# Attention folds and node scores of a two-layer relational graph network: small products placed as pairs in two column groups of the PE array

## The chip, the cores and the metric

The kernel runs on one NeuronCore of a Trainium2 chip. A core has TensorE (PE in the profile; PEld is its weight load), VectorE (DVE), ScalarE (ACT), GpSimd (POOL), a sync engine that issues transfers (SP) and 16 DMA engines. PE writes to PSUM, eight banks of 128 partitions by 512 f32 words; the other engines copy from there to SBUF. The metric is the device time of one execution in microseconds (us), median of several runs; lower is better.

## The reference

The network has 1250 nodes of 768 features, 20,000 edges with one of three types, and three message-passing layers. Cut to what matters here:

```python
h = relu(layernorm(x));  x = x + gcn(h, W0)               # layer 0
h = relu(layernorm(x))
for each of two attention layers (4 heads, then 1):
    xr = einsum('nd,rdf->rnf', h, W)                      # three relations
    qi = xr[etype, dst] @ q ;  kj = xr[etype, src] @ k    # node scores
    alpha = leaky_relu(qi + kj, 0.2)
    a = softmax of alpha over the edges with the same dst
    h = segment_sum(a * xr[etype, src], dst) + b          # elu after the first
x = x + h
```

The kernel never forms `xr @ q`. It folds the vectors into the weights (`W[r] @ q` and `W[r] @ k`, 768 numbers for each relation and head), and gets the node scores as a product of the node features with the folded vectors. The fold of the first attention layer (four heads) is done on PE; that of the second is done on DVE. In the few words given for the change, the fold is called the second layer's: of the three message-passing layers, the first attention layer is the second.

## The kernel before, in words

Edges are sorted by destination on the chip, in slots of 128, two slots a pair. Nodes are in `NT` = 10 tiles of 128, features in `KT` = 6 blocks of 128. `ps` is all of PSUM as one tile of eight banks. All orders are written out by hand: each engine has its own program, and semaphores link them. Two places matter.

**The fold on PE (lines 1111 to 1136).** Each of three weight matrices (order `FOLDS`) comes in six blocks, in all 18 steps `q`. `turn_block(q)` transposes six 128x128 tiles of a block into PSUM (L1106), ACT copies them to one of two buffers `wt` (L568), and `wq_tile(q)` multiplies (L1135): stationary are 8 columns (query and key vectors, 4 heads each), moving are the 768 columns of `wt` in two halves `h` of 384, one to bank 4 and one to bank 5. PE issues the transposes of `q + 1` ahead of the products of `q`. After six blocks ACT copies both banks' 8 rows to `wqT` (L573), and `fold(r)` transposes that back (L1117). Twelve steps come at the very start, ahead of the first projection; six come in a second stage behind it, just ahead of the first gather loop (L1287).

**The node scores (lines 1239 to 1257).** `by_query(l, g)` takes two tiles of nodes: for each of the six feature blocks it multiplies the 24 folded columns (6 in the second attention layer) with 256 columns of `hT`, and adds up in one bank (L1248). ACT copies the 24x256 result to `qkT` (L637), and `by_node` transposes its two halves (L1257). There are five groups `g` in each attention layer. They stand inside the aggregation loops of the layer before (`to_features`): PE runs the products of node tile `j`, then transposes tile `j - 2`, and at every second tile runs a group of `by_query` first. In the first attention layer `by_node` follows at once, in the second one tile later, save for the last group. The groups 3 and 4 come after the last gather loop.

In these gather loops (L1287 for layer 0, L1353 for the first attention layer) POOL gathers rows to a ring of eight slots, SP relays that they came, DVE writes a one-hot matrix `zw` for a slot (L904, L1083), and PE multiplies it with the row; each step waits for its semaphore.

Every product in float32 with a 128-row contraction shows in the trace as two records of PE and two of PEld: 36 products of L1135 are 72 records, and 60 of L1248 are 120.

Of the kernel before, what the change touches and what calls it, by code (L numbers as in the profile page):

```python
# [15 lines left out]
ACT = mybir.ActivationFunctionType  # L16
# [8 lines left out]
P = 128  # L25
# [3 lines left out]
R = 3  # L29
NT = (N + P - 1) // P  # L30
NP_ = NT * P
KT = D // P
# [5 lines left out]
PAIR = 2 * P  # L38
# [14 lines left out]
QT_BANK, QV_BANK, QV_AT = {1: 4, 2: 6}, {1: 5, 2: 7}, 256  # L53
# [10 lines left out]
HALF = D // 2  # L64
# [18 lines left out]

FOLDS = (2, 1, 0)
NF = 2 * KT


GROUPS_AT = {nt: ((3 * nt,), (3 * nt + 1, 3 * nt + 2)) for nt in range(6)}
# [12 lines left out]
def gnn_kernel(nc, x, src, dst, edge_type, W0, b0, W1, q1, k1, b1, W2, q2, k2, b2, out):  # L101
    HEADS = {1: 4, 2: 1}
# [11 lines left out]
    with ExitStack() as ctx:  # L114
# [6 lines left out]
        ps = ctx.enter_context(nc.psum_tensor("ps", [P, 8, 512], F32))  # L121
# [3 lines left out]
        hT = sb("hT", [P, KT, NP_])  # L125
# [8 lines left out]
        qkT = zw[:, 1, 0, 1:3, :].rearrange("p h c -> p (h c)")  # L134
# [50 lines left out]
        wt = [temp(D) for _ in range(2)]  # L185
        wqT = temp(D, F32, 2 * HEADS[1])
# [15 lines left out]
        wqk = {l: sb(f"wqk{l}", [P, KT, 2, R * HEADS[l]]) for l in (1, 2)}  # L202
        qk1 = sb("qk1", [P, KT, 2, HEADS[1]])
# [55 lines left out]
        wqT_in, wq_folded = sem("wqT_in"), sem("wq_folded")  # L259
# [29 lines left out]
        qt_ready, qt_copied = sem("qt_ready"), sem("qt_copied")  # L289
# [275 lines left out]
        def _(act):  # L565
# [4 lines left out]

            def keep_folded(r):
                act.wait_ge(wt_used, KT * (r + 1))
                nc.scalar.activation(wqT.rearrange("p (a c) -> p a c", a=2), ps[0:2 * HEADS[1], 4:6, 0:HALF], ACT.Copy).then_inc(wqT_in, 1)  # L573

            def keep_transposed(q):
                if q >= 2:
# [41 lines left out]
            for i in range(R):  # L618
                H = HEADS[1]
                c = HALF + i % 2 * KT * 2 * H  # L620
# [13 lines left out]

            def keep_by_query(l, g):
                act.wait_ge(qt_ready, (l - 1) * NT // 2 + g + 1)
                nc.scalar.activation(qkT[0:2 * R * HEADS[l], :], ps[0:2 * R * HEADS[l], QT_BANK[l], 0:PAIR], ACT.Copy).then_inc(qt_copied, 1)  # L637

            for nt in range(NT):
                if nt % 2 == 0 and nt >= 2:  # L640
# [20 lines left out]
            for l in (1, 2):  # L661
# [5 lines left out]
                for r in range(R):  # L667
                    for nt in range(NT):
                        b = nt % 2
# [430 lines left out]
        def _(pe):  # L1100
            mm = nc.tensor.matmul
# [9 lines left out]
            def fold(r):  # L1111

                w = 2 * HEADS[1]
                pe.wait_ge(wqT_in, r + 1)
                for k in range(KT):
                    c = HALF + (r % 2 * KT + k) * w
                    last = nc.tensor.transpose(ps[:, 5 - r // 2, c:c + w], wqT[:, k * P:(k + 1) * P], ident[0:w, 0:w])  # L1117
                last.then_inc(wq_folded, 1)
# [8 lines left out]
            def wq_tile(q):  # L1127
                f = q % KT
                if q == 0:
                    pe.wait_ge(s_qk, 32)  # L1130
                if q == KT:
                    fold(0)
                pe.wait_ge(t_free, (q if q < NF else q + NT) + 1)
                for h in range(2):
                    last = mm(ps[0:2 * HEADS[1], 4 + h, 0:HALF], qk1[:, f, :, :].rearrange("p a h -> p (a h)"), wt[q % 2][:, h * HALF:(h + 1) * HALF], start=(f == 0), stop=(f == KT - 1))  # L1135
                last.then_inc(wt_used, 1)

            def sort_group(g):
# [100 lines left out]
            def by_query(l, g):  # L1239

                if l == 1:
                    pe.wait_ge(wq_copied, R)
                    pe.wait_ge(t_free, NW + NT + 2 * g + 2)
                else:
                    pe.wait_ge(h2_ready, 2 * g + 2)
                w = 2 * R * HEADS[l]
                for k in range(KT):
                    last = mm(ps[0:w, QT_BANK[l], 0:PAIR], wqk[l][:, k, :, :].rearrange("p a q -> p (a q)"), hT[:, k, g * PAIR:(g + 1) * PAIR], start=(k == 0), stop=(k == KT - 1))  # L1248
                last.then_inc(qt_ready, 1)

            def by_node(l, g):
# [42 lines left out]
            for l in (1, 2):  # L1294
# [22 lines left out]
                for r in range(R):  # L1317
# [3 lines left out]
                    for nt in range(NT):  # L1321
                        project(r, nt)
                        for n in MAX_AT.get(r * NT + nt, ()):
                            if n < NT:
# [4 lines left out]
                                for b in range(2):  # L1329
                                    for h in range(H):  # L1330
                                        c = 4 * 512 + (b * H + h) * P
# [53 lines left out]
```

## Time and profile before

| | us |
|---|---|
| median of three runs (1623.75 to 1627.2) | 1625.71 |
| the profiled execution | 1627.17 |
| span in its trace | 1625.4 |
| PE busy | 1477.0 (91%) |
| PE weight loads busy | 879.7 (54%) |
| POOL busy | 998.0 (61%) |
| DVE busy | 901.6 (55%) |
| ACT busy | 271.7 (17%) |

The profile is of one execution. Its busy time of PE counts overlapping records once. A record of a product begins when it starts to stream and ends when its last result is in PSUM, so products that follow each other closely have overlapping records; the step from one to the next is less than the duration of one. Where an instruction waits, its row gives the idle time before it and what ended it.

### The profile page before, as it was taken

The page shows a single profiled execution, that of the slowest core. Times are in us where ns is not written, and L with a number is a line of the kernel's source. Part 1 is how long each engine was busy: PE and PEld are TensorE (multiplying, and loading weights), DVE is VectorE, ACT ScalarE, POOL GpSimd, SP SyncE. Part 2 cuts the span into 40 slices and gives each one's busy share as a digit, 9 for nine tenths or more (in the row PEclk, how much of TensorE's full clock was granted, in tenths as well). Part 3 has the DMA queues.
Part 4 walks back from the last instruction along what each step waited for, and adds up shares of the span by engine and source line. Part 5 has one row for each costly group of instructions (what it writes and reads, how often), then busy time and mean ns, then how long its engine had stood idle before and what let it go on. Part 6 is the DMA issues. An engine that isn't in the chain of part 4 may idle for free.

```text
span 1625.4 us, 24584 instructions
## 1 busy us (share of the span) xinstructions
PE 1477.0 (91%) x6326; PEld 879.7 (54%) x6330; DVE 901.6 (55%) x2002; ACT 271.7 (17%) x696; POOL 998.0 (61%) x1112
## 2 busy tenths in 40 slices
PE   4988999999978999999699999868996999799996
PEld 2554655555556555666455555445553656455553
DVE  8577732334454878888688888505334445223333
ACT  1554310000011333322100123420110001000000
POOL 1489367665527777873277776427656662677673
PEclk9988999999986999899799999968998999899999
DMA  8300399898822122111388888711131111889898
GB/s 305 127 20 21 99 319 306 291 316 294 268 65 66 51 77 82 41 41 41 111 302 288 292 259 258 241 25 31 50 108 31 41 50 50 266 299 306 284 303 265
DMA packets 86810, 271.78 MB, mean 167 GB/s; under 512 B 32156, under 2 KB 32531, under 8 KB 86743
## 3 DMA queue, kind: packets, MB, share of 16 engines
q0 software_dynamic: 51072, 199.44, 39.0%
q1 hardware_dynamic: 34807, 65.62, 11.3%
q10 hardware_dynamic: 864, 5.90, 1.0%
q8 instruction: 34, 0.56, 0.1%
q14 instruction: 33, 0.27, 0.1%
HBM read 239.28 MB, written 31.62 MB: 167 GB/s over the span
## 4 chain that ended last, share of the span: by engine, by line
PE 65%; DMA 11%; POOL 9%; issue 7%; DVE 6%; ACT 1%; DVEq 0%; SPq 0%; POOLq 0%; PEldq 0%; ACTq 0%
PE ps L1353 12%; PE ps L1287 12%; PE ps L1314 12%; DMA ring<-keys,idxr 7%; POOL ring L517 7%; PE ps L1355 6%; PE ps L1356 6%; PE ps L1185 5%; PE ps L1231 3%; DMA ring<-rows,idxr 2%; PE ps L1248 2%; PE ps L1135 2%; PE ps L1106 2%; PE ps L1148 1%; DVE hn L1012 1%
## 5 line engine op out<-in xcount | busy, mean ns | idle before, releaser
L1314 PE MATMUL ps<-wreg,hT 128*128 128x384 f32 x1440 | 484.1, 498 | 7.3 <-PEq L1307 6.6
L517 POOL DMA_INDIRECT ring<-keys,idxr x312 | 323.2, 1036 | 191.4 <-DMA ring<-keys,idxr 72.7
L486 POOL DMA_INDIRECT ring<-rows,idxr x304 | 299.7, 986 | 180.6 <-PEq L1342 66.5
L1314 PEld LDWEIGHTS ps<-wreg,hT 128*128 128x128 f32 x1440 | 279.2, 195 | 200.8 <-issue 21.2
L1353 PE MATMUL ps<-ring,zw 128*128 x664 | 222.2, 493 | 13.0 <-DVE zw L1083 12.6
L1287 PE MATMUL ps<-ring,zw 128*128 x664 | 220.4, 493 | 7.9 <-DVE zw L904 7.9
L486 POOL DMA_INDIRECT ring<-rows,idx x152 | 145.4, 956 | 98.1 <-PE ps L1287 67.3
L1353 PEld LDWEIGHTS ps<-ring,zw 128*128 128x128 f32 x664 | 124.6, 191 | 104.9 <-issue 29.8
L1081 DVE TENSOR_TENSOR ring<-ring,al x166 | 159.0, 958 | 36.4 <-SPq L404 24.7
L1287 PEld LDWEIGHTS ps<-ring,zw 128*128 128x128 f32 x664 | 126.6, 192 | 96.3 <-issue 13.9
L1086 DVE TENSOR_SCALAR zw<-iota_f,tl,al 128x128 f32<-128x128 f32 x166 | 61.5, 372 | 155.8 <-PE ps L1356 133.3
L1355 PE MATMUL ps<-ring,zw 128*128 x332 | 137.3, 496 | 10.1 <-DVE zw L1086 10.1
L904 DVE TENSOR_SCALAR zw<-iota_f,tl,ring 128x128 f32<-128x128 f32 x166 | 58.5, 358 | 158.5 <-PE ps L1287 135.4
L471 POOL TENSOR_SCALAR stT<-iota_h,stT 125x128 f16<-125x128 f16 x160 | 106.6, 685 | 56.2 <-PE ps L1150 28.2
L1356 PE MATMUL ps<-ring,zw 128*128 x332 | 135.9, 491 | 0.0
L1012 DVE TENSOR_TENSOR hn<-al,hn 128x1024 f32 x83 | 101.7, 1225 | 38.1 <-POOL al L535 14.5
L1018 DVE TENSOR_TENSOR hn<-hn,al 128x256 f32 x83 | 35.6, 429 | 142.2 <-POOL al L535 126.2
L1015 DVE TENSOR_TENSOR zw<-zw,hn 128x1024 f32<-128x1024 f32 x83 | 101.7, 1226 | 2.9
L1355 PEld LDWEIGHTS ps<-ring,zw 128*128 128x128 f32 x332 | 62.6, 192 | 54.6 <-issue 16.1
L1356 PEld LDWEIGHTS ps<-ring,zw 128*128 128x128 f32 x332 | 63.7, 192 | 44.8 <-issue 1.5
L1185 PE MATMUL ps<-ring,hT 128*128 128x384 f32 x240 | 87.8, 522 | 0.0
L684 ACT ACTIVATE stage<-ps 128x384 f32<-128x384 f32 x60 | 29.5, 491 | 276.8 <-PE ps L1314 276.8
(189 smaller groups left out, 1363.4 us busy)
## 6 DMA issues: line engine op xcount, KB each, us to landing
wreg<-in_L_gnn_W SPq DMA_DIRECT2D x11, 2304.0 KB, 9.7
rows<-stage SPq DMA_DIRECT2D x30, 386.0 KB
rows<-stage SPq DMA_DIRECT2D x30, 384.5 KB, 2.8
stT<-targets_row ACTq DMA_DIRECT2D x6, 960.0 KB
ring<-keys,idxr POOLq DMA_INDIRECT x312, 2.4
ring<-rows,idxr POOLq DMA_INDIRECT x304, 4.6
rows<-stT SPq DMA_DIRECT2D x10, 384.0 KB, 2.8
xs<-in_x SPq DMA_DIRECT2D x3, 1152.0 KB, 13.1
```

The lines of the kernel that those rows point to most:

```text
L471: nc.gpsimd.tensor_scalar(oh_tg[:, c % PB, :], iota_h[0:EP, 0:P], dloc[:, c:c + 1], None, ALU.is_equal).then_inc(tg_in, 1)
L486: nc.gpsimd.indirect_dma_start(ring[:, t % (2 * RING), 0:WIDTH[l]], None, rows[l], bass.IndirectOffsetOnAxis(idx[:, t:t + 1], 0)).then_inc ...
L517: nc.gpsimd.indirect_dma_start(kb[:, n % KSEMS, t % KB, 0:4], None, keys[l], bass.IndirectOffsetOnAxis(idxr[:, t:t + 1], 0)).then_inc(k_in ...
L1012: V.tensor_tensor(scored[:, :, 0:H, :], scores_at(i, 0, H, 2).rearrange("p (b h) -> p b h", b=2).unsqueeze(3).to_broadcast([P, 2, H, P]), ...
L1015: V.tensor_tensor(run, run, scored[:, :, 0:H, :], ALU.max).then_inc(m_chain[l], 1)
L1081: V.tensor_tensor(row, row, scores_at(i, b, H).unsqueeze(2).to_broadcast([P, H, ROW // H]), ALU.mult).then_inc(rows_scaled, 1)
L1185: last = mm(ps[:, 4 - 2 * (nt % 2) + h, 0:HALF], hT[:, k, nt * P:(nt + 1) * P], w0s[:, k, h * HALF:(h + 1) * HALF], start=(k == 0), stop=( ...
L1287: last = mm(ps[:, 2 * (j % 2) + a, 0:HALF], zw[:, 0, b, 0, :], row_at(i, b, a * HALF, (a + 1) * HALF), start=False, stop=False, skip_group ...
L1314: last = mm(ps[:, 2 * (nt % 2) + h, 0:HALF], hT[:, k, nt * P:(nt + 1) * P], wreg[:, r % 2, k, h * HALF:(h + 1) * HALF], start=(k == 0), st ...
L1353: last = mm(ps[:, 2 * (j % 2) + a, 0:2 * W], zw[:, 0, b, 0, :], row_at(i, b, a * 2 * W, (a + 1) * 2 * W), start=False, stop=False, skip_gr ...
L1355: mm(ps[:, 2 * (j % 2), 0:HALF], zw[:, 0, b, 0, :], row_at(i, b, 0, HALF), start=False, stop=False, skip_group_check=True)
L1356: last = mm(ps[:, 2 * (j % 2) + 1, 0:HALF + 1], zw[:, 0, b, 0, :], row_at(i, b, HALF, D + 1), start=False, stop=False, skip_group_check=True)
```

## The change

The two products of each pair now write different partitions of PSUM, and so lie in different groups of columns of the PE array: the first at partition 0, the second at 64. In the fold these are the two halves of 384 columns, which exist already. In the node scores the one product of 256 columns becomes two of 128, one for each node tile. All other products keep their place. As a consequence the two ACT copies can't take both results in one instruction: L573 and L637 each become two of half the width. The copy of the folds now signals after each half, and `fold` waits for both; the copy of the scores signals once, after its second half. The built program showed a 32-column tile of the array for these products before too, at position 0; now half of them are at column 64.

```diff
+QK_AT = (0, 64)
+WQ_AT = (0, 64)
...
             def keep_folded(r):
                 act.wait_ge(wt_used, KT * (r + 1))
-                nc.scalar.activation(wqT.rearrange("p (a c) -> p a c", a=2), ps[0:2 * HEADS[1], 4:6, 0:HALF], ACT.Copy).then_inc(wqT_in, 1)
+                for h in range(2):
+                    nc.scalar.activation(wqT[:, h * HALF:(h + 1) * HALF], ps[WQ_AT[h]:WQ_AT[h] + 2 * HEADS[1], 4 + h, 0:HALF], ACT.Copy).then_inc(wqT_in, 1)
...
             def keep_by_query(l, g):
-                nc.scalar.activation(qkT[0:2 * R * HEADS[l], :], ps[0:2 * R * HEADS[l], QT_BANK[l], 0:PAIR], ACT.Copy).then_inc(qt_copied, 1)
+                for b, c in enumerate(QK_AT):
+                    last = nc.scalar.activation(qkT[0:2 * R * HEADS[l], b * P:(b + 1) * P], ps[c:c + 2 * R * HEADS[l], QT_BANK[l], 0:P], ACT.Copy)
+                last.then_inc(qt_copied, 1)
...
             def fold(r):
-                pe.wait_ge(wqT_in, r + 1)
+                pe.wait_ge(wqT_in, 2 * (r + 1))
...
                 for h in range(2):
-                    last = mm(ps[0:2 * HEADS[1], 4 + h, 0:HALF], ...
+                    last = mm(ps[WQ_AT[h]:WQ_AT[h] + 2 * HEADS[1], 4 + h, 0:HALF], ...
...
                 for k in range(KT):
-                    last = mm(ps[0:w, QT_BANK[l], 0:PAIR], wqk[l][:, k, :, :].rearrange("p a q -> p (a q)"), hT[:, k, g * PAIR:(g + 1) * PAIR], start=(k == 0), stop=(k == KT - 1))
+                    for b, c in enumerate(QK_AT):
+                        last = mm(ps[c:c + w, QT_BANK[l], 0:P], wqk[l][:, k, :, :].rearrange("p a q -> p (a q)"), hT[:, k, (2 * g + b) * P:(2 * g + b + 1) * P], start=(k == 0), stop=(k == KT - 1))
```

On PE, the first group of node scores of the first attention layer, between two gather loops (`hT` holds node features, `wqk` folded vectors, `hn` normalised nodes), before:

```order
L1248 MATMUL ps<-hT,wqk 24x256 x6
L1257 MATMUL ps<-ident,zw 128x24 x2
L1277 MATMUL ps<-ident,hn 128x128 x6
L1211 MATMUL ps<-zero 128x8 x2
L1283 UNCONDITIONAL_BRANCH
```

and now:

```order
L1254 MATMUL ps<-hT,wqk 24x128 x12
L1263 MATMUL ps<-ident,zw 128x24 x2
L1283 MATMUL ps<-ident,hn 128x128 x6
L1216 MATMUL ps<-zero 128x8 x2
L1289 UNCONDITIONAL_BRANCH
```

Six products have become twelve of half the width; nothing else has moved on PE. The fold's products keep their count and shape there.

On ACT, the first stage of the folds (`stT` holds `wt` and `wqT`), before:

```order
L568 ACTIVATE stT<-ps 128x768 x7
L573 ACTIVATE stT<-ps 8x768
L568 ACTIVATE stT<-ps 128x768 x5
L573 ACTIVATE stT<-ps 8x768
L568 ACTIVATE hT<-ps 128x6x128 x2
```

and now:

```order
L570 ACTIVATE stT<-ps 128x768 x7
L576 ACTIVATE stT<-ps 8x384 x2
L570 ACTIVATE stT<-ps 128x768 x5
L576 ACTIVATE stT<-ps 8x384 x2
L570 ACTIVATE hT<-ps 128x6x128 x2
```

Each copy of a folded result is two instructions; all others stand where they stood.

## Rows read from the trace of the kernel before

**Rows 1.** The page: span, and the lines of the chain that ended last.

```profile
span 1625.4 us, 24584 instructions
...
PE ps L1353 12%; PE ps L1287 12%; PE ps L1314 12%; DMA ring<-keys,idxr 7%; POOL ring L517 7%; PE ps L1355 6%; PE ps L1356 6%; PE ps L1185 5%; PE ps L1231 3%; DMA ring<-rows,idxr 2%; PE ps L1248 2%; PE ps L1135 2%; PE ps L1106 2%; PE ps L1148 1%; DVE hn L1012 1%
```

**Rows 2.** Line 1135: records, ns minimum/median/maximum, first and last start, forms.

```profile
L1135 PEld LDWEIGHTS ps<-stT,qk x72: 85/90/138, 20.8 to 214.2; 128*8 128x8 f32 x72
L1135 PE MATMUL ps<-stT,qk x72: 486/486/847, 20.8 to 214.5; 128*8 128x384 f32 x72
```

**Rows 3.** Timeline of a fold step: start us, us, engine, line, operation, [idle before].

```profile
24.40 1.46 PE L1135 MATMUL ps<-stT,qk 128*8 128x384 f32 x4
24.73 0.09 PEld L1135 LDWEIGHTS ps<-stT,qk 128*8 128x8 f32 x1 [0.23 <-issue]
25.79 0.87 PE L1106 MATMUL ps<-ident,wreg 128*128 128x128 f32 x6
```

**Rows 4.** Windows: stretch, length, busy PE, PEld, DVE, ACT, POOL, granted clock, DMA.

```profile
37.00:41.00 4.00, 4.00 (x14) 1.55 (x13) 3.79 (x11) 1.61 (x2) 0.00 (x0) 0.57 0.02 6
```

**Rows 5.** Timeline at the end of the first fold stage.

```profile
46.21 1.26 DVE L827 TENSOR_SCALAR hn<-xs,mv,rstd 128x768 f32<-128x768 f32 x2
...
53.22 0.80 ACT L573 ACTIVATE stT<-ps 8x768 f32<-8x768 f32 x1 [1.80 <-PE ps L1135]
54.08 0.54 PE L1117 MATMUL ps<-ident,stT 8*128 8x8 f32 x6 [0.89 <-ACT stT L573]
54.54 0.88 PE L1106 MATMUL ps<-ident,hn 128*128 128x128 f32 x6
```

**Rows 6.** Timeline at the end of the second fold stage.

```profile
202.05 0.27 ACT L613 ACTIVATE tlT<-ps 128x128 bf16<-128x128 f32 x1
202.21 0.26 ACT L614 ACTIVATE tlT<-ps 52x128 bf16<-52x128 f32 x1
...
214.73 0.60 DVE L904 TENSOR_SCALAR zw<-iota_f,tl,ring 128x128 f32<-128x128 f32 x2 [4.46 <-SPq L404]
...
216.40 6.05 PE L1287 MATMUL ps<-ring,zw 128*128 x18
```

**Rows 7.** Line 1248 between 366 and 560 us: records as in Rows 2.

```profile
L1248 PEld LDWEIGHTS ps<-hT,wqk x60: 98/103/103, 371.8 to 471.0; 128*24 128x24 f32 x60
L1248 PE MATMUL ps<-hT,wqk x60: 376/379/397, 371.8 to 471.2; 128*24 128x256 f32 x60
```

**Rows 8.** Timeline around group 1 of the first attention layer's scores.

```profile
409.31 2.77 PE L1248 MATMUL ps<-hT,wqk 128*24 128x256 f32 x12
...
411.62 0.59 DVE L904 TENSOR_SCALAR zw<-iota_f,tl,ring 128x128 f32<-128x128 f32 x2
...
413.54 1.86 PE L1287 MATMUL ps<-ring,zw 128*128 x5
```

**Rows 9.** Timeline around group 2.

```profile
441.94 0.60 DVE L904 TENSOR_SCALAR zw<-iota_f,tl,ring 128x128 f32<-128x128 f32 x2 [2.32 <-SPq L404]
442.45 2.84 PE L1287 MATMUL ps<-ring,zw 128*128 x8 [0.74 <-DVE zw L904]
...
449.45 3.79 PE L1287 MATMUL ps<-ring,zw 128*128 x11
...
451.27 0.35 DVE L904 TENSOR_SCALAR zw<-iota_f,tl,ring 128x128 f32<-128x128 f32 x1 [3.71 <-SPq L404]
```

**Rows 10.** Timeline behind group 0 of the second attention layer, and of groups 3 and 4.

```profile
968.14 1.66 ACT L708 ACTIVATE etmp<-ps,b1c 128x128 f32<-128x128 f32 x6 [0.43 <-PE ps L1277]
...
1051.35 4.32 PE L1248 MATMUL ps<-hT,wqk 128*6 128x256 f32 x12 [5.03 <-DVE hT L1062]
...
1053.02 0.14 PEld L1248 LDWEIGHTS ps<-hT,wqk 128*6 128x6 f32 x1 [0.29 <-issue]
1053.45 0.14 PEld L1248 LDWEIGHTS ps<-hT,wqk 128*6 128x6 f32 x1 [0.29 <-issue]
...
1066.54 5.25 PE L1248 MATMUL ps<-hT,wqk 128*6 128x256 f32 x12 [9.03 <-DVE hT L1062]
```

More of the change, by code:

```diff
@@ L1134, in wq_tile @@
                 for h in range(2):
-                    last = mm(ps[0:2 * HEADS[1], 4 + h, 0:HALF], qk1[:, f, :, :].rearrange("p a h -> p (a h)"), wt[q % 2][:, h * HALF:(h + 1) * HALF], start=(f == 0), stop=(f == KT - 1))
+                    last = mm(ps[WQ_AT[h]:WQ_AT[h] + 2 * HEADS[1], 4 + h, 0:HALF], qk1[:, f, :, :].rearrange("p a h -> p (a h)"), wt[q % 2][:, h * HALF:(h + 1) * HALF], start=(f == 0), stop=(f == KT - 1))
                 last.then_inc(wt_used, 1)
```

## The prediction

> **What bounds the kernel now.** I read the chain that ended last first. Its lines give L1248 and L1135, the two lines that the change touches, 2% of the span each [rows 1]. That is some 32 us each of 1625.4 with the rounding (1.5 to 2.5% would be 24 to 40), and about all the time these lines stream, so nearly every changed product stands on the path. Then the records of each line [rows 2, 7], for the step from one product to the next, and the timeline at both ends of each stage, for what is late once PE comes sooner. In the fold a step of q takes 24.40 to 25.79 for four records and then the transposes [rows 3]: PE waits for nothing but its own order there, and ACT's copy lies beside it.
>
> **The unit.** A fold record takes 486 ns [rows 2] but the next begins 0.33 us behind it (24.40 to 24.73, the load that goes with it [rows 3]); the rest is the fill of the array and lies under its follower. So the four records of a step of q are 4 x 0.325 = 1.30 us. In the node scores twelve records take 2.77 us with one of them 379 ns [rows 7, 8]: (2.77 - 0.38) / 11 = 0.217 us a step.
>
> **What two column groups can save.** The trace of before shows no product at column 64, so this is bounded from both sides. One end: nothing overlaps, saving 0. Other end: each pair takes the time of one product, saving half of all streaming. I take a value between, from how a float32 product is made up: two records, on the same column group. I assume that products start in the order in which they are issued and that two on one column group can't stream together. With A and B the two groups, the order is A1 A2 B1 B2. A2 waits for A1, B1 starts with A2, B2 waits for B1. A lone pair then takes three units in place of four; a row of pairs takes two units a pair, plus one at its end, since the next A1 goes beside B2. No row here shows it; it is nearer to the full end for the scores than for the folds.
>
> The Trainium skill, "TensorE: Matmul & The Clock Gate", section "Part 3: Packing small matmuls", says that products in different column groups run together, that they start and end in program order, and that a packed set takes one product's duration and some 4 ns for each further tile. Taken for whole float32 products it gives the full end, which is a rival below; its statement on order is what I assume, and no run here has shown either yet.
>
> **First fold stage, 12 steps.** Eight lone steps at full clock save one unit: 8 x 0.325 = 2.6. The first step and the one after PE's pause at 36 us run at about half clock (0.57 granted in that window [rows 4], the longest record 847 ns [rows 2]), with a unit of twice 0.325, so 0.65; but if the clock rises at the same moment as now, the transposes behind it get the slow time instead, which leaves 0.33. I take 0.45 each, 0.9. The last two steps stand together with a short wait for ACT in between: 0.6. Together 4.1. The two folded copies become two each: 8x768 took 0.80 us [rows 5]. Two back-to-back ACT copies of 128 columns start 0.16 us apart and last 0.27 [rows 6], so a split costs about 0.05 (bounds: 0 by overlap, 0.26 by the longest spacing in the trace for such a width, 1.66 us for six [rows 10]). 4.1 - 0.1 = 4.0. What is late next: the transposes of `hn` at 54.54, whose input DVE began at 46.21 and had at 47.5 [rows 5]. So a shift of up to 7 us passes on. Behind it the sort and the first projection are linked to PE through semaphores on each column, so all of it moves by the same 4.0.
>
> **Second fold stage, 6 steps.** They would save 4 x 0.325 + 0.6 - 0.05 = 1.85. But the gather loop waits for DVE's one-hot: that began at 214.73 [rows 6], and PE's first use of such a one came 0.51 us after its start at 441.94 [rows 9]. So PE can't start before 215.24, and now does at 216.40 [rows 6]: 1.15 counts.
>
> **Node scores of the first attention layer, 5 groups.** Before 12 x 0.217 = 2.60. Now 24 records of half the unit: 13 x 0.108 = 1.41, saving 1.19. A floor of issue stands against this: six tiny products at L1117, each with a load, take 0.54 us, less 0.2 for the last one's fill (my estimate), so 0.066 each [rows 5]; 24 x 0.066 = 1.6, saving 1.0. I take 1.1. Cover ahead: at group 1 DVE's one-hot started at 411.62 and is usable at 412.13, PE starts at 413.54 [rows 8]: room for 1.4. Group 0 stands alike. At group 2 the third slot's one-hot starts only at 451.27, held by the gather, so it is usable at 451.78; PE gets to it at 449.45 + 8 x 0.325 = 452.05 [rows 9]: only 0.3 counts. Groups 3 and 4 have no loop behind them. 4 x 1.1 + 0.3 = 4.7, less five split copies of 0.06: 4.4.
>
> **Node scores of the second attention layer.** Groups 0 to 2 lie in the loop at full clock, and their copies are read one tile later, so are free: 3.3. Group 3 takes 4.32 and group 4 5.25 us, as PE had idled (5.03 and 9.03 us) and its step is 0.43 us, 1053.02 to 1053.45, the lower of its two clock levels [rows 10]. Now 13 x 0.214 + 0.17 = 2.95 each. Group 3 saves 1.4 less 0.3 for transposes behind it that come before the clock rises: 1.1. Group 4 saves 2.3, less 0.06: 2.2. Sum 6.6.
>
> **Sum.** 4.0 + 1.15 + 4.4 + 6.6 = 16.2 us off the profiled execution's 1627.17 (span 1625.4 and 1.8 around it), so 1611.0. That execution stands 1.5 above the median of the runs; the same saving from 1625.71 gives 1609.6, the forecast. Its own range is 1602 to 1616.
>
> The Trainium skill, "TensorEngine Tiling (Array Packing)", section "Key Properties", has a change of tiling mode drain the array. The 0.17 us of idle that PE's loads show between transposes and fold products would be such a change and stays, since the mode was the same before; so the sum is the same by it.
>
> **Rivals.**
> (a) Every product's two records overlap with the other product's, the full end. Folds then save two units a step (about 8.2 in the first stage, still 1.15 in the second by its cap), scores 0.1 more a group: about 21.5 saved, 1604. For it: nothing in the trace says that a second record must wait. Against it: same-group records step at 0.33 now. 0.07.
> (b) The overlap works, but the gather loops give the time back, PE meeting rows that haven't come. For it: group 2's slack of 0.3, one-hots held by SP's relay [rows 9]. Against it: 1.4 of room at group 1 [rows 8]. Then the five groups inside the loops give nothing (3.3 and 2.5 lost): 10.4 saved, 1615. 0.11.
> (c) Nothing overlaps: two products that both read all 128 rows stream one after the other. The change then doesn't do what it is said to do; 24 half steps take what 12 did. Left are the split copies, 3 x 0.05 and 6 x 0.06 = 0.5, at most nine of 0.26 = 2.3: 1626.2 to 1628. For it: no row shows an overlap. 0.17.
> (d) Slower: weight loads of one column group can't run under products of the other. Now each load of 103 ns [rows 7] hides under a product on its own group; if it stood free, a group of scores would take 24 x (0.108 + 0.103) = 5.1 in place of 2.6, +2.5 in eight groups, and +3.4 in the two at the low clock (24 x (0.214 + 0.14) = 8.5 against 5.1); a fold step +4 x 0.09 = 0.36 [rows 2], 18 times. 20 + 6.8 + 6.5 + 0.5 = 34 slower, 1659. It decides from 0.05 us of exposed load on each record of the scores, where 24 of them eat the 1.19 saved. For it: the loads double in number while the streams halve. Against it: 103 ns would still fit under a stream of 108. 0.15.
> The same page's section "Part 3: Packing small matmuls" has loads overlap with products in flight only where the row group differs, and here both groups use all rows: that is this rival. For a single column group the trace disagrees, as loads start under running products at 24.73 [rows 3].
>
> **Chances.** Forecast 0.50, (a) 0.07, (b) 0.11, (c) 0.17, (d) 0.15. I call faster or slower what differs by over 0.2% (3.3 us), about what a measurement of this kernel can tell from no change: faster 0.68 (the forecast, (a) and (b)), same 0.17, slower 0.15. The range is 1602 to 1628: it takes in (b) and (c) and leaves out (d) and the far end of (a).
>
> **What would show it.** In the profile after, the four records of a lone fold step lie within about 1.14 us from first start to last end in place of 1.46, and the second and third start together; a score group is about 1.6 to 1.75 long in place of 2.77 with 24 records of some 270 ns; the first gather loop starts some 5 us sooner; PE's busy time falls by more than 15 us. Score groups over 2.7 us long would make the prediction wrong by (c), loads with idle time between them and products by (d). If the groups are short but the aggregation loops longer by as much, it is (b).

## The result, and the profile after

The changed kernel took 1606.98 us in the median of four runs (1604.7 to 1619.93), beside 1626.45 for the kernel before (four runs): ratio 0.9891, 95% interval 0.9861 to 0.9921. Run again later beside 11 runs of the kernel before it came to 1608.81 (six runs, 1602.91 to 1613.88) against 1622.92: 0.9913, 0.9886 to 0.994. So it is faster, by 19.5 us the first time and 14.1 the second, by the medians; the forecast was 1609.6. Executions of one program here spread over 10 us and more (29 runs of the kernel before: 1620.12 to 1634.32), so a trace and a median can differ by several us.

The page of the changed kernel, to compare with [rows 1]:

```profile
span 1605.3 us, 24837 instructions
...
PE 1453.7 (91%) x6446; PEld 878.0 (55%) x6450; DVE 901.0 (56%) x2002; ACT 274.0 (17%) x709; POOL 1000.9 (62%) x1112
...
PE ps L1293 12%; PE ps L1320 12%; PE ps L1359 12%; DMA ring<-keys,idxr 8%; POOL ring L519 8%; PE ps L1361 6%; PE ps L1362 6%; PE ps L1190 5%; DMA ring<-rows,idxr 3%; PE ps L1111 1%; PE ps L1236 1%; PE ps L1153 1%; PE ps L1254 1%; DVE zw L1020 1%; DVE hn L1017 1%
```

PE is busy 23.3 us less. The fold line (L1140 now) has left the list of the chain and the score line (L1254 now) has gone from 2% to 1%. The records of both lines, against [rows 2] and [rows 7] (the first two of the fold, the next two of the scores between 350 and 480 us; ns minimum/median/maximum):

```profile
L1140 PEld LDWEIGHTS ps<-stT,qk x72: 85/88/95, 20.8 to 204.0; 128*8 128x8 f32 x72
L1140 PE MATMUL ps<-stT,qk x72: 486/489/847, 20.8 to 204.3; 128*8 128x384 f32 x72
```

```profile
L1254 PEld LDWEIGHTS ps<-hT,wqk x120: 98/103/103, 367.3 to 458.3; 128*24 128x24 f32 x120
L1254 PE MATMUL ps<-hT,wqk x120: 269/273/290, 367.3 to 458.4; 128*24 128x128 f32 x120
```

A fold record is as long as it was; loads are too. What changed is when they start. The timeline of a fold step, against [rows 3], and under it the same step asked for up to 25.0 us only:

```profile
24.95 0.10 PEld L1140 LDWEIGHTS ps<-stT,qk 128*8 128x8 f32 x4 [0.17 <-issue]
24.95 0.82 PE L1140 MATMUL ps<-stT,qk 128*8 128x384 f32 x4
...
25.70 0.87 PE L1111 MATMUL ps<-ident,wreg 128*128 128x128 f32 x6
```

```profile
24.95 0.49 PE L1140 MATMUL ps<-stT,qk 128*8 128x384 f32 x2
```

All four loads lie in the first 0.10 us, two records have started by 25.0 (at 24.951 and 24.957) and the other two follow a unit of 0.325 later (25.276 and 25.283): 2 x 0.325 + 0.17 = 0.82, in place of 1.46. The overlap is full. It is not that the second product waits for the first to reach its second record, as I had assumed: it starts ahead of it.

Scores, group 1 of the first attention layer, against [rows 8]:

```profile
401.96 1.50 PE L1254 MATMUL ps<-hT,wqk 128*24 128x128 f32 x24
...
403.51 0.55 ACT L641 ACTIVATE zw<-ps 24x128 f32<-24x128 f32 x2 [15.88 <-PE ps L1254]
404.11 0.30 PE L1263 MATMUL ps<-ident,zw 24*128 24x24 f32 x2 [0.65 <-ACT zw L641]
...
404.27 0.59 DVE L909 TENSOR_SCALAR zw<-iota_f,tl,ring 128x128 f32<-128x128 f32 x2
...
405.10 1.21 PE L1293 MATMUL ps<-ring,zw 128*128 x3
```

24 records take 1.50 us, twelve units of 0.11 and the fill. The gather loop's products begin 3.14 us behind the group's start, before 4.23 [rows 8]: 1.1 us saved. PE waits for the copy 0.65 us, 0.2 more than before (0.46).

What the trace shows of the stages, as PE reaches them (before / after, us): transposes of `hn` 54.54 / 50.93; end of the sort and projection (the two transposes ahead of the second fold stage) 201.46 / 194.71; first gather loop 216.40 / 208.51; score group 0 371.82 / 367.26; score group 1 409.31 / 401.96; last group 468.81 / 457.19; group 3 of the second attention layer 1051.35 / 1034.81; end 1625.4 / 1605.3. PE gains 3.6, then 3.1 more in the sort, 1.1 in the second fold stage; then it loses 3.3 in the first gather loop. Group 0 of the scores is reached 4.6 us sooner, and 15.5 are gained behind it. Not all of that is the change's: from group 0 to group 1 PE gains 2.8 us, of which group 0 itself gives 1.1. The same interval before, now, and in the kernel with column groups in the scores alone (below):

```profile
371.82:409.31 37.49, 34.96 (x120) 20.24 (x119) 15.69 (x37) 2.00 (x3) 21.95 (x23) 0.95 0.88 293
```

```profile
367.26:401.96 34.70, 32.00 (x131) 19.59 (x130) 15.09 (x35) 2.16 (x4) 21.39 (x23) 1.00 0.91 312
```

```profile
368.69:405.07 36.38, 33.67 (x131) 20.33 (x130) 15.72 (x37) 2.16 (x4) 21.44 (x23) 0.95 0.89 299
```

At the same granted clock of 0.95 the interval is 1.11 us shorter, as the group's saving has it; the other 1.7 us go with a clock of 1.00, and what set it in that execution is open.

The loss of 3.3 us has a cause in the rows. Windows (columns as in [rows 4]) of the first 10 us of the first gather loop, before and after:

```profile
216.40:226.40 10.00, 10.00 (x33) 5.97 (x34) 2.53 (x7) 0.42 (x3) 7.10 (x9) 1.00 0.90 301
```

```profile
208.50:218.50 10.00, 9.99 (x23) 5.67 (x23) 1.74 (x6) 0.00 (x0) 5.81 (x7) 0.72 0.82 255
```

Before, PE came from the folds straight into the loop, at full clock. Now it comes early, waits 1.99 us for the first one-hot, and starts at the lower of its two levels: 23 records in place of 33. All traces of this study agree: the three kernels with the folds as before have 33 or 34 records and a granted clock of 1.00 in these 10 us, and the seven executions with column groups in the folds and nothing put into the wait have 22 to 27 records and 0.69 to 0.85.

The first fold stage shows the same twice over. PE's rows around its pause, before and after:

```profile
30.97 1.46 PE L1135 MATMUL ps<-stT,qk 128*8 128x384 f32 x4
36.62 0.87 PE L1106 MATMUL ps<-ident,wreg 128*128 128x128 f32 x6 [4.18 <-issue]
37.41 2.73 PE L1135 MATMUL ps<-stT,qk 128*8 128x384 f32 x4
40.08 1.21 PE L1106 MATMUL ps<-ident,wreg 128*128 128x128 f32 x6
```

```profile
28.06 0.82 PE L1140 MATMUL ps<-stT,qk 128*8 128x384 f32 x4
34.34 1.54 PE L1111 MATMUL ps<-ident,wreg 128*128 128x128 f32 x6 [5.47 <-issue]
...
42.27 1.42 PE L1140 MATMUL ps<-stT,qk 128*8 128x384 f32 x4
43.61 0.88 PE L1111 MATMUL ps<-ident,wreg 128*128 128x128 f32 x6
```

The pause has grown from 4.18 to 5.47 us. Before, the first six transposes behind it were still fast (0.87 us), and the low clock lay between 37.4 and about 41 us. Now it begins with the transposes at 34.34 (1.54 us) and lasts to about 43. The line of the register loads says what the pause is (PE's sequencer, ns as above), before and after:

```profile
L344 PEldq TENSOR_LOAD <-bounds x10: 294/304/482, 29.9 to 36.0; - x10
```

```profile
L346 PEldq TENSOR_LOAD <-bounds x10: 294/302/494, 27.7 to 33.7; - x10
L346 PEldq FUSED_REGOPS  x10: 146/146/165, 28.2 to 34.1; - x10
```

Ten loads of the tile bounds, each with what goes with it, take 6.6 us of sequencer time (27.7 to 34.3 now, 29.9 to 36.5 before), some 0.66 us each. They begin while the array still has work queued: 2.5 us ahead of the end of its products before (32.43), 1.2 us now (28.88). So shorter products hide less of them: 2.3 us of the 3.5 that the five steps ahead of the pause had won pass on.

### The profile page after: what moved, and what is told of

It is laid out like the page before. It is cut to its first block, busy times and chain, and to the rows that moved or that the text cites. A ratio compares the mean times of both kernels' runs of the same rounds, so it can differ in the third digit from the quotient of the medians.

```text
span 1605.3 us, 24837 instructions
## 1 busy us (share of the span) xinstructions
PE 1453.7 (91%) x6446; PEld 878.0 (55%) x6450; DVE 901.0 (56%) x2002; ACT 274.0 (17%) x709; POOL 1000.9 (62%) x1112
## 4 chain that ended last, share of the span: by engine, by line
PE 61%; DMA 14%; POOL 10%; issue 7%; DVE 5%; ACT 1%; DVEq 1%; SPq 0%; POOLq 0%; ACTq 0%; PEldq 0%
PE ps L1293 12%; PE ps L1320 12%; PE ps L1359 12%; DMA ring<-keys,idxr 8%; POOL ring L519 8%; PE ps L1361 6%; PE ps L1362 6%; PE ps L1190 5%; DMA ring<-rows,idxr 3%; PE ps L1111 1%; PE ps L1236 1%; PE ps L1153 1%; PE ps L1254 1%; DVE zw L1020 1%; DVE hn L1017 1%
## 5 line engine op out<-in xcount | busy, mean ns | idle before, releaser
L519 POOL DMA_INDIRECT ring<-keys,idxr x312 | 319.2, 1023 | 189.1 <-DMA ring<-keys,idxr 73.6
L488 POOL DMA_INDIRECT ring<-rows,idxr x304 | 303.7, 999 | 168.8 <-PEq L1348 60.9
L1017 DVE TENSOR_TENSOR hn<-al,hn 128x1024 f32 x83 | 101.7, 1225 | 35.4 <-POOL al L537 15.5
L1023 DVE TENSOR_TENSOR hn<-hn,al 128x256 f32 x83 | 35.6, 429 | 143.8 <-POOL al L537 127.8
L659 ACT ACTIVATE hn<-iota_f,tlb 128x128 f32<-128x128 f32 (+1 forms) x166 | 56.8, 393 | 119.2 <-DVE hn L1017 105.7
```

The costliest lines, as they stand in the source:

```text
L488: nc.gpsimd.indirect_dma_start(ring[:, t % (2 * RING), 0:WIDTH[l]], None, rows[l], bass.IndirectOffsetOnAxis(idx[:, t:t + 1], 0)).then_inc ...
L519: nc.gpsimd.indirect_dma_start(kb[:, n % KSEMS, t % KB, 0:4], None, keys[l], bass.IndirectOffsetOnAxis(idxr[:, t:t + 1], 0)).then_inc(k_in ...
L1017: V.tensor_tensor(scored[:, :, 0:H, :], scores_at(i, 0, H, 2).rearrange("p (b h) -> p b h", b=2).unsqueeze(3).to_broadcast([P, 2, H, P]), ...
```

## The experiments

### Each half of the change alone

`e1_folds` has the column groups in the folds alone, `e2_scores` in the scores alone. `e2_scores` has the fold lines of the kernel before; the edit of `e1_folds` against the changed kernel is:

```diff
-                for b, c in enumerate(QK_AT):
-                    last = nc.scalar.activation(qkT[0:2 * R * HEADS[l], b * P:(b + 1) * P], ...)
-                last.then_inc(qt_copied, 1)
+                nc.scalar.activation(qkT[0:2 * R * HEADS[l], :], ps[0:2 * R * HEADS[l], QT_BANK[l], 0:PAIR], ACT.Copy).then_inc(qt_copied, 1)
...
-                    for b, c in enumerate(QK_AT):
-                        last = mm(ps[c:c + w, QT_BANK[l], 0:P], ...)
+                    last = mm(ps[0:w, QT_BANK[l], 0:PAIR], ...)
```

> Column groups in the folds alone; node scores as before. Theory (the overlap is full, two records of A with two of B, and what it saves passes on): a fold step stays 0.82 us of PE, the score groups are back at 2.77. The first stage gives 3.6 us earlier transposes of hn, the second is cut by the wait for the first one-hot and by the low clock behind that wait, so 4 to 9 us faster than before in all (the 20 us of the whole change less 11 to 13 for the scores). Rival (the folds' saving is lost in the sort, and the scores make up the gain): within 2 us of before.

> Column groups in the node scores alone; folds as before. Theory: each group 1.50 us in place of 2.77, about 1.05 saved net of the longer wait for ACT in the five of the first attention layer, 1.27 in three of the second, 1.6 and 2.3 in the last two: 5.3 + 3.8 + 3.9 = 13 us faster at most, 10 to 13. Rival (gather loops give back what is saved inside them): 6 to 8 us.

Measured: folds alone 1623.32 us (12 runs) against 1625.63 of the kernel before (29 runs), ratio 0.9991 (0.9975 to 1.0008): 2.3 us by the medians, at most 4.1 by the interval, and not told from nothing. Scores alone 1612.89 (6 runs): 0.9927 (0.9906 to 0.9948), 12.7 us. Together 15, which agrees with the 14.1 of the second measurement of the whole. So the scores carry nearly all of the gain. My range of 4 to 9 us for the folds was too high but for its lowest end; the rival's size, within 2 us or so, fits. Its reason, that the sort eats the saving, does not (see the pause below).

The same loss at the start of the gather loop is seen here: `hn` is transposed 5.1 us sooner than before in the profiled execution (49.45 us), and the loop's first 10 us have a low clock (26 records in place of 33):

```profile
209.80:219.80 10.00, 9.99 (x26) 5.84 (x27) 2.19 (x7) 0.00 (x0) 6.83 (x9) 0.84 0.89 300
```

Single traces do not place the rest of what is missing. Over the five executions with two column groups in the folds, the pause in place and nothing put into the waits, group 0 of the scores starts at 368.2 us in the mean (366.6 to 370.9), over the three with the folds as before at 371.6 (368.7 to 374.2): 3.4 us sooner, with a spread as large. So part of the folds' saving seems to be left there, and 2.3 us and 3.4 us can't be told apart.

### Is it the overlap, or the shorter product?

```diff
                 for k in range(KT):
-                    last = mm(ps[0:w, QT_BANK[l], 0:PAIR], wqk..., hT[:, k, g * PAIR:(g + 1) * PAIR], ...)
+                    for b in range(2):
+                        last = mm(ps[0:w, QT_BANK[l], b * P:(b + 1) * P], wqk..., hT[:, k, (2 * g + b) * P:(2 * g + b + 1) * P], ...)
```

> The kernel before with the node scores split into twelve products of 128 columns, all in the one column group at partition 0, side by side in the bank, with one ACT copy. Theory (the gain is the overlap of two column groups): no gain, a group takes 24 x 0.108 + 0.17 = 2.77 us, as with twelve records of 0.217, total within 2 us of before. Rival (the shorter products are the gain, since fill and loads hide better): groups clearly under 2.77 us. Rival (a short product exposes its load): groups of 24 x 0.2 = 5 us, 20 us slower.

This kernel leaves out part of the score sums (the sums of both halves lie in one bank at the same partitions); instructions and shapes are those intended. It took 1628.26 us (10 runs), ratio 1.0008 (0.9987 to 1.0029). A group:

```profile
374.17 2.80 PE L1249 MATMUL ps<-hT,wqk 128*24 128x128 f32 x24
```

2.80 us for the same 24 records that take 1.50 in two column groups. Halving the product costs nothing and gains nothing; the column group is what gains. It also prices rival (c): had nothing overlapped, the time would have stayed.

### Does the order of issue matter?

```diff
-                for k in range(KT):
-                    for b, c in enumerate(QK_AT):
+                for b, c in enumerate(QK_AT):
+                    for k in range(KT):
```

> The whole change, but each score group issues its six products of column group 0 first, then the six of column group 64, in place of taking turns. Theory (products start in the order of issue, and two overlap only where neighbours in that order lie in different groups): only the one pair at the seam overlaps, a group takes 11 product times, 22 x 0.108 + 0.17 = 2.55 us or more, and total is about 11 us slower than the changed kernel. Rival (PE picks products of a free column group out of its queue): groups stay at 1.50 us and the total is that of the changed kernel, 1607.

1623.61 us (10 runs), ratio 0.9978 (0.996 to 0.9997): 2.0 us under the kernel before that was measured beside it, where the changed kernel was 14.1 under its own. So some 12 us are lost, nearly all of the scores' gain. A group:

```profile
370.93 2.39 PE L1254 MATMUL ps<-hT,wqk 128*24 128x128 f32 x24
```

The loads between 371.815 and 371.83 alone; two begin there within 2 ns (371.818 and 371.820):

```profile
371.82 0.10 PEld L1254 LDWEIGHTS ps<-hT,wqk 128*24 128x24 f32 x2
```

2.39 us. Against 2.80 without overlap that is 0.41, or four records of 0.109 that overlap at the seam. I had expected two. The starts show how: eight records stand alone, 0.11 us apart; the first of the second set starts at 371.822, 6 ns behind the ninth of the first set (371.816), and the last three of the first set only follow at 371.925, 372.035 and 372.144. So PE took products of the free column group ahead of some that had to wait, but only over a few records: products that are to overlap have to stand next to each other. The Trainium skill, "TensorE: Matmul & The Clock Gate", section "Part 3: Packing small matmuls", has products start strictly in program order; this trace does not agree, by those three records. Nor does the lone fold step, where the second product starts 0.32 us ahead of the first one's second record.

### Four column groups in the folds

```diff
-WQ_AT = (0, 64)
+WQ_AT = (0, 32, 64, 96)
+QUART = D // 4
...
-                for h in range(2):
-                    last = mm(ps[WQ_AT[h]:WQ_AT[h] + 2 * HEADS[1], 4 + h, 0:HALF], ...)
+                for h in range(4):
+                    last = mm(ps[WQ_AT[h]:WQ_AT[h] + 2 * HEADS[1], 4 + h // 2, h % 2 * QUART:(h % 2 + 1) * QUART], ...)
```

> The changed kernel once more, beside the next three on one chip, since its first result had four runs only. Theory of additive parts: folds alone gave about 2 us and scores alone about 12.5, so this gives 14 to 16 us less than before, 1610 to 1612. Rival (the parts help each other, as the first four runs had it): 19 less, 1607.

> The changed kernel with the folds' 768 columns in four quarters of 192, at columns 0, 32, 64 and 96, and four ACT copies. Theory (groups overlap freely up to four, but what PE saves in the folds now meets waits: ten register loads in the first stage, the first one-hot and a low clock in the second): a fold step takes 0.50 us in place of 0.82, and the total stays within 2 us of the changed kernel. Rival (a third and fourth group don't overlap, moving data being the limit): the step stays 0.82. Rival (what folds save counts): 4 us or more faster than the changed kernel.

The changed kernel came to 1608.81, as the additive theory had it. Four groups in the folds came to 1604.3 (6 runs), ratio 0.9878 (0.9853 to 0.9902), against 0.9913 (0.9886 to 0.994) of the changed kernel. The intervals overlap, so 4.5 us is the best guess and not shown; neither the theory (within 2 us) nor the rival (4 us or more) is decided. The step is 0.51 us as expected, and the wait for the first one-hot grows:

```profile
207.05 0.51 PE L1141 MATMUL ps<-stT,qk 128*8 128x192 f32 x8 [0.52 <-ACT stT L571]
209.04 0.80 PE L1123 MATMUL ps<-ident,stT 8*128 8x8 f32 x6 [1.48 <-ACT stT L577]
...
213.12 1.64 PE L1294 MATMUL ps<-ring,zw 128*128 x2 [3.12 <-DVE zw L910]
```

3.12 us of wait in place of 1.99, and 1.48 for the four copies in place of 1.09.

### The pause in the first fold stage

```diff
-                if q == KT:
-                    bnd = load_bounds(pe)
...
                     last.then_inc(p_ready, 1)
+                    if h == 0:
+                        j = nt + 1
+                        pe.wait_ge(bounds_ready, 1)
+                        bnd.append(pe.value_load(bounds[0:1, j:j + 1], ...))
```

> The changed kernel with PE's ten register loads of the tile bounds moved from the middle of the first fold stage to behind the products of each of the ten node tiles' first half in the projection, where PE's sequencer runs ahead of the array. Theory (the pause of 5.5 us, 28.9 to 34.3, is the sequencer's ten loads of 0.64 us, and the low clock until 43.6 follows from it): no pause, transposes of hn start when DVE's hn is there, at 47.5 to 48, in place of 50.9, so 3 us faster in total at most. Rival (the pause is the wait for the second weight matrix): it stays. Rival (the sort takes up the difference): total as the changed kernel.

The pause is gone, so it was the loads. But the total is 1610.43 (6 runs), ratio 0.9923 (0.9898 to 0.9947): no gain over the changed kernel is seen, though the intervals would hide one of 3 us. PE:

```profile
41.99 0.54 PE L1122 MATMUL ps<-ident,stT 8*128 8x8 f32 x6 [1.09 <-ACT stT L576]
46.91 1.54 PE L1111 MATMUL ps<-ident,hn 128*128 128x128 f32 x6 [4.38 <-DVE hn L832]
```

The folds are done 8.5 us sooner, then PE waits 4.38 us for `hn` and enters the sort at the low clock, 1.54 us for six transposes in place of 0.88. `hn` at 46.91 is 4.0 us sooner than at 50.93, and the end of the sort is at 195.94, 1.2 later. The sort stage in four traces, by windows from the transposes of `hn` to its end:

```profile
54.54:201.46 146.92, 133.08 (x624) 78.70 (x623) 100.48 (x371) 70.67 (x189) 103.89 (x153) 0.91 0.16 57
```

```profile
50.93:194.71 143.78, 130.32 (x625) 76.54 (x624) 100.48 (x371) 70.66 (x189) 103.75 (x153) 0.93 0.16 58
```

```profile
46.91:195.94 149.03, 135.18 (x622) 80.35 (x623) 104.16 (x388) 70.72 (x189) 103.73 (x153) 0.89 0.13 46
```

```profile
54.36:198.04 143.68, 130.25 (x625) 76.50 (x624) 100.48 (x371) 70.63 (x189) 103.74 (x153) 0.93 0.17 58
```

These are the kernel before, the changed one, this one (where some of DVE's earlier work falls into the stage, 388 instructions in place of 371), and scores alone, whose sort and folds are those of the kernel before. Length goes with the granted clock: 0.93, 0.91, 0.89. The last row shows that the 3.1 us which the changed kernel's trace gained in the sort is not the change's: a kernel without column groups in its folds had them too.

The other traces say more. With the folds as before the stage took 143.7, 146.9 and 149.4 us in three kernels; with two column groups in them, and the pause in place, 143.7 to 143.8 (four executions), 146.6 to 146.7 (three) and 149.5 (one). The same three lengths come in both, so the sort does not take up what the folds save. Over these eight executions `hn` is transposed at 50.30 us in the mean (48.95 to 51.26), over the three with the folds as before at 54.34 (54.12 to 54.54): 4.0 us sooner. What sets the clock of an execution in the sort I did not test; it stays open.

### Keeping PE busy in its waits

```diff
             wq_tile(NW - 1)
+            def fill(n):
+                for _ in range(n):
+                    mm(ps[:, 6, :], zero16[:, 0:P], zero16[:, 0:512], start=True, stop=True)
+            fill(4)
             fold(R - 1)
+            fill(8)
```

> The changed kernel with products of zeros in PE's two waits ahead of the first gather loop: 4 of 512 columns while ACT copies the fold, 8 more while the first one-hot is awaited (0.215 us each at full clock, to a bank nobody reads). Theory (the low clock behind that wait, granted 0.72 in the first 10 us, cost 2.7 us of the folds' saving): granted clock near 1.00 there, 2 to 2.7 us faster in total. Rival (the gather is the limit at the loop's start): clock up, total the same.

> The filler kernel once more, since it came out 8 us under the changed kernel of the same call where its trace accounts for 2.6 (in the first 10 us of the gather loop 31 records in place of 23). Theory (the rest was chance between executions): 1605 to 1607 here. Rival (it was real): 1600 to 1601.

The first 10 us of the gather loop now:

```profile
208.00:218.00 10.00, 9.92 (x31) 5.96 (x32) 2.95 (x8) 0.00 (x0) 7.57 (x8) 1.00 0.94 327
```

Full clock, and 31 records in place of 23: 8 x 0.325 = 2.6 us, the expected size. From its first product to score group 0 the loop takes 155.7 us here and 155.8 in the repeat, 158.75 in the changed kernel and 155.42 in the kernel before: the loss of 3.3 us is undone but for 0.3. So the low clock was its cause, and the waits were what it followed. In total 1600.43 (5 runs), ratio 0.9867 (0.984 to 0.9893), and again 1602.29 (6 runs), 0.9876 (0.9846 to 0.9906), measured at another time. That is 6.5 to 8.4 us under the changed kernel's 1608.81, of which the trace accounts for 2.6 to 3.0. The repeat fell between my two expectations. The ratios' intervals reach the changed kernel's, so what the rows show stands and the rest does not.

The second set of fillers stands in the waits ahead of the last two score groups:

```diff
+                if l == 2 and g >= 3:
+                    pe.wait_ge(divided, 9)
+                    fill_tail({3: 32, 4: 64}[g])
...
+                if l == 2:
+                    fill_tail(12)
                 pe.wait_ge(q16_ready, l)
```

> The filler kernel with more products of zeros (256 columns, to a bank nobody reads) in PE's long waits ahead of groups 3 and 4 of the second attention layer's scores (32 and 64) and behind the last (12). Theory (these groups take 2.73 us in place of 1.50 only for the low clock, and transposes and the next products of zeros after them are slow too): groups 1.50 us each, 1.2 + 1.2 us, 1.2 to 2 for what stands behind them: 3 to 4 us faster than the filler kernel. Rival (the fillers delay ACT or PE by as much): no gain.

In the changed kernel, and then in this one (in both, the first row is group 3):

```profile
1034.81 2.73 PE L1254 MATMUL ps<-hT,wqk 128*6 128x128 f32 x24 [5.01 <-DVE hT L1067]
1037.47 1.54 PE L1283 MATMUL ps<-ident,hn 128*128 128x128 f32 x6
```

```profile
1030.13 1.48 PE L1268 MATMUL ps<-hT,wqk 128*6 128x128 f32 x24 [1.52 <-DVE hT L1067]
1031.54 0.88 PE L1297 MATMUL ps<-ident,hn 128*128 128x128 f32 x6
...
1033.27 7.15 PE L1253 MATMUL ps<-zero 128*128 128x256 bf16 x64
1042.45 1.82 PE L1268 MATMUL ps<-hT,wqk 128*6 128x128 f32 x24 [2.03 <-DVE hT L1067]
...
1048.18 2.28 PE L1228 MATMUL ps<-zero 128*128 128x512 bf16 x5 [0.22 <-issue]
```

Group 3 and its transposes are fast. Group 4 gets 1.82 us; a wait of 2.03 was left ahead of it. The 12 fillers behind it ran at the low clock (2.74 us, where 32 had taken 3.66), and what follows starts 5.73 us behind the group's start, 5.72 in the changed kernel: what the group saved is lost there. In total 1600.75 (6 runs), ratio 0.9862 (0.9833 to 0.9891), 1.5 us under the filler kernel measured beside it: half of what I expected, and within the spread.

### Four column groups in the scores, and all together

```diff
-QK_AT = (0, 64)
+QK_AT = (0, 32, 64, 96)
...
                     for b, c in enumerate(QK_AT):
-                        last = mm(ps[c:c + w, QT_BANK[l], 0:P], ...)
+                        last = mm(ps[c:c + w, QT_BANK[l], 0:P // 2], wqk..., hT[:, k, (4 * g + b) * P // 2:(4 * g + b + 1) * P // 2], ...)
```

> The changed kernel with the score groups in four products of 64 columns at columns 0, 32, 64 and 96, and four ACT copies of 64 columns. Theory (up to four groups overlap, and 96 records with their loads can still be issued at under 10 ns each): a group takes 12 x 0.055 + 0.17 = 0.83 us in place of 1.50, less 0.2 us of longer copies where PE waits for them: 4 to 6 us faster than the changed kernel's 1608.8. Rival (loads bind: with 24 columns each and four at once they can't hide under 54 ns of stream): group stays near or above 1.5 us, no gain or slower.

> All of it together: four column groups in folds and scores, and both sets of fillers. Theory (each saves what its trace shows, and the fills keep the clock up): 1593 to 1598. Rival (four groups give nothing more, as their savings turn into waits): the same as with fillers alone and two groups.

Four groups in the scores: 1598.12 us (6 runs), ratio 0.9841 (0.9811 to 0.9871), 10.7 under the changed kernel's 1608.81 of another time, where I expected 4 to 6. A group (six feature blocks of four products, so 48 records and not the 96 that I wrote):

```profile
368.92 0.87 PE L1254 MATMUL ps<-hT,wqk 128*24 128x64 f32 x48
369.96 0.90 ACT L641 ACTIVATE zw<-ps 24x64 f32<-24x64 f32 x4 [16.68 <-PE ps L1254]
370.91 0.30 PE L1263 MATMUL ps<-ident,zw 24*128 24x24 f32 x2 [1.12 <-ACT zw L641]
```

0.87 us in place of 1.50, and loads of 24 columns still hide. PE waits 1.12 us for the copies in this group and 1.01 or 1.02 in later ones, in place of 0.65. So where the transposes follow at once a group gains 0.16 to 0.26 net, and 0.63 in three others; the two slow groups of the second attention layer (1.47 us each in place of 2.73) gain 1.3 and 0.9. By these rows all groups give some 5 us, so part of the 10.7 is spread again. That this kernel is faster than the changed one is shown, as the intervals of the ratios lie apart (0.9871 and 0.9886), though measured at two times.

All together came to 1595.31 us (6 runs, 1592.22 to 1603.39), ratio 0.9843 (0.9811 to 0.9875): the lowest median of this study, 28.7 us under the kernel before measured beside it (25.5 by the ratio), and faster than both kernels of the document. Over four groups in the scores alone it isn't proved (the ratios are the same). In the trace of all together PE still waits 1.69 us for the first one-hot behind the fillers, and the next 10 us have a granted clock of 1.00 and 31 records.

## Why the prediction was right

**Time and side.** 1609.6 forecast, 1606.98 and 1608.81 measured; own range 1602 to 1616. The forecast's case came true: groups overlap, and the time falls. That the sum came within 3 us is partly luck, as its parts were off in both directions: folds 5.15 forecast and 2.3 measured alone, scores 11.0 and 12.7, and the overlap itself was fuller than assumed.

**Where the changed lines stand.** Reading the two lines' shares of the chain as "nearly all of it on the path" was right for the scores (12.7 us passed on of the 13 that their rows gave at most). For the folds it was right of their time, but waits and a low clock took part of its place.

**The unit.** Wrong: the step "A2 waits for A1, B1 starts with A2", and the premise under it, that products start in the order of issue. The two products start 0.01 us apart and their second records follow together, so a lone pair takes two units, not three. That is the full end, rival (a), to which I gave 0.07. A fold step saved 0.64 us, twice the 0.325 of the sum.

**First fold stage, 4.0.** The trace has 3.6, and eight executions 4.0 in the mean, but as two errors that cancel. Full overlap would have given about 8; the pause took 1.3 (4.18 to 5.47 us), the low clock from 34 to 43 us most of the rest. I had counted the pause as fixed in length, where the loads in it are: what was queued ahead of them hid 2.5 us and now hides 1.2. The split of the folded copy cost 0.2 us (a wait of 1.08 or 1.09 in place of 0.89), not 0.05.

**The sort moves with it.** Single traces can't show it, as the stage differs by up to 6 us with the granted clock (0.90 to 0.93), more than the shift itself. But it took the same three lengths with either kind of folds, so nothing speaks against it.

**Second fold stage, 1.15.** 14.94 us before and 13.80 now from end of sort to first gather product: 1.14. The cap by DVE's one-hot was right. What I did not see is the price behind it, a wait of 1.99 us that put PE to its lower clock and cost 2.6 to 3.0 us, as the filler kernel shows. With it the second stage loses. So the folds' 5.2 us were mis-sized, 2.3 measured (0.9991, interval 0.9975 to 1.0008).

**Scores of the first attention layer, 4.4.** Up to the gather loop's next product group 1 saves 1.09, with 1.27 on PE and 0.2 of longer wait for ACT (I had 1.1 and 0.06). The floor of issue of 0.066 us a record did not hold: 24 records in two groups start some 0.053 us apart (1.50 us less the 0.27 of the last one, over 23), and 48 in four groups 0.014 (0.87 less 0.2, over 47). The cap of 0.3 at group 2 did not show either: from it to group 3 took 16.45 us before and 15.35 now (445.22 to 461.67, 435.77 to 451.12), and the third slot's one-hot, which the gather held to 451.27, now starts at 440.73 behind a wait for PE alone. The trace's 7.1 us between group 0 and the last are more than these groups' own 4.4, 1.7 of it by the clock of one interval as said above.

**Scores of the second attention layer, 6.6.** Group 3 saves 1.6 and group 4 2.5 (4.32 and 5.25 us in [rows 10], 2.73 each now) against 1.4 and 2.3; the transposes behind group 3 cost 0.66 and not 0.3, and the products of zeros behind group 4 now run at the low clock (five in 2.34 us), which I had not counted. Near.

**Rivals.** (b) is refuted for the scores (12.7 us of scores alone), but something like it is what happened to the folds. (Its sum leaves out six groups, three of each layer, where its words say five.) (c) and (d) are refuted: scores alone are faster, a group is short, and four loads lie within 0.10 us. The Trainium skill, "TensorE: Matmul & The Clock Gate", section "Part 3: Packing small matmuls", lets loads overlap only across row groups; taken as (d) took it, that does not hold in these rows, where 24 loads lie under the records of a group of 1.50 us.

## What to carry to other kernels

Products with few output rows, of the same contraction, can be issued next to each other at output partitions 0 and 64, or 0, 32, 64 and 96, and stream at once, in float32 too; issued one set after the other, only a few at the seam do. Read what a saving runs into before counting it: here, time taken from PE just ahead of a wait was given back, and more, as the clock fell in the wait. If a wait can't be filled with work, products of zeros in it can keep what stands behind it fast, as they did ahead of the gather loop and of group 3.

## What was not expected of the hardware

- Full overlap of float32 products of two column groups (0.82 us in place of 1.46), and of four (0.51 for eight records of 192 columns; 0.87 for 48 of 64).
- A seam of just four overlapping records where two column groups were issued one after the other, and at it a record that starts ahead of three that were issued before it.
- Waits of 1.09 and 1.99 us with 0.7 us of small products between them were followed by the low clock (0.72 granted over the next 10 us, 23 records in place of 33); the kernel before had the first wait only, of 0.89 us. Behind 1.9 us of zeros a wait of 1.69 us was not (1.00, 31 records).
- The same sort stage at 143.7 to 149.5 us, with the granted clock between 0.93 and 0.90, in executions of programs that are alike in it.
